# Expert stage: image rows as column pairs, per-expert low weights and bias brought by DMA

## The reference

```
scores = softmax(mean(x, axis=1) @ Wg.T)          # one choice per sample, 3 experts
sel    = top_1(scores)
h      = gelu(x @ W1[sel] + b1[sel])              # 192 -> 768
y      = h @ W2[sel] + b2[sel]                    # 768 -> 192
out    = x + y * scores[sel]
```

## Time and profile before

| what | us |
|---|---|
| median of 3 runs (1023.57 to 1028.31) | 1025.52 |
| the profiled execution's own time | 1024.34 |
| its span, first to last instruction | 1022.5 |
| PE / DVE / ACT busy over the span | 704.2 / 870.8 / 709.0 |
| start of the first product of sample 0 | 857.83 |
| PE wait for DMAs in the expert stage, once | 6.9 |

### The profile page before, as it was taken

One profiled execution on the slowest core, in us unless ns is written; L12 is line 12 of the kernel. 1 busy time (PEld: TensorE's weight loads), 2 busy tenths in 40 slices (PEclk: granted clock), 3 DMA queues, 4 the chain that ended last, 5 costly groups with the idle time before them and its releaser, 6 DMA issues. The chain is left out here.

```text
span 1022.5 us, 23611 instructions
## 1 busy us (share of the span) xinstructions
PE 704.2 (69%) x6531; PEld 475.1 (46%) x6532; DVE 870.8 (85%) x2388; ACT 709.0 (69%) x1376; POOL 171.0 (17%) x276
## 2 busy tenths in 40 slices
PE   3783387747888467766677756677635384999997
PEld 3562144434655333333344333343323254999896
DVE  6888997888888889999999999999978854677766
ACT  0345365966888799999898999999944393554553
POOL 5851320006665100000000000000005530000000
PEclk9986598988999787789777797777857697999999
DMA  8000000001111111111111111111021004455452
GB/s 259 3 2 0 0 1 1 0 0 37 37 37 37 40 28 25 24 25 28 24 25 24 25 26 24 24 24 24 13 105 64 18 1 155 144 192 199 163 193 90
DMA packets 84272, 54.72 MB, mean 54 GB/s; under 512 B 53704, under 2 KB 83176, under 8 KB 83976
## 3 DMA queue, kind: packets, MB, share of 16 engines
q1 hardware_dynamic: 83208, 54.11, 17.4%
q0 software_dynamic: 1024, 0.13, 0.2%
HBM read 11.90 MB, written 3.76 MB: 15 GB/s over the span
## 5 line engine op out<-in xcount | busy, mean ns | idle before, releaser
L1365 DVE SCALAR_TENSOR_TENSOR expo<-expo,con,pow 128x153 f32<-128x153 f32 x480 | 146.2, 376 | 0.7 <-ACT expo L1275 0.7
L1149 PE MATMUL at_rem<-word,ident_half 128*128 128x459 f16 x160 | 68.7, 430 | 104.6 <-ACT expo L1275 102.5
L1275 ACT ACTIVATE expo<-at_rem,con 128x459 f32<-128x459 f32 x160 | 98.8, 645 | 17.3 <-PE at_rem L1150 13.0
L952 DVE TENSOR_REDUCE rs_ends<-rs_banks 128x770 f32 (+1 forms) x96 | 89.2, 958 | 12.7 <-PE rs_banks L924 10.3
L1401 DVE CUSTOM_DVE_ANT_0 weight_top<-weight_top,line 128x2448 uint16<-128x2448 uint16 x64 | 85.6, 1352 | 6.4 <-ACT line L1267 4.5
L873 ACT ACTIVATE rs_banks<-rs_banks 128x770 f32<-128x770 f32 x96 | 74.3, 796 | 22.9 <-PE rs_banks L916 21.8
L1149 PEld LDWEIGHTS at_rem<-word,ident_half 128*128 128x128 f16 x160 | 15.7, 98 | 152.7 <-ACT expo L1275 146.7
L1238 ACT ACTIVATE word<-at_banks 128x459 uint8<-128x459 f32 x160 | 79.6, 560 | 8.5 <-PE at_banks L779 5.5
L1231 ACT ACTIVATE pT_all<-at_pT 128x768 bf16<-128x768 int16 (+3 forms) x160 | 78.9, 562 | 8.3 <-PE at_pT L1173 2.5
L1907 ACT ACTIVATE qk<-e_p,b1s 128x153 f32<-128x153 f32 x192 | 58.7, 393 | 28.4 <-PE e_p L1868 27.3
L1868 PE MATMUL e_p<-X,qk 128*128 (+1 forms) x960 | 71.8, 234 | 7.3 <-DMA qk<-vt 6.9
(11 more groups left out here) (387 smaller groups left out, 2040.7 us busy)
## 6 DMA issues: line engine op xcount, KB each, us to landing
qk<-vt SPq DMA_DIRECT2D x64, 384.0 KB, 3.1
rs_kb<-qk SPq DMA_DIRECT2D x128, 28.7 KB, 1.9
kb<-qk SPq DMA_DIRECT2D x128, 28.7 KB, 1.9
patches<-in_patches SPq DMA_DIRECT2D x4, 768.0 KB
vi<-vt SPq DMA_DIRECT2D x32, 96.0 KB, 2.0
out<-vi SPq DMA_DIRECT2D x32, 96.0 KB, 1.9
pj_w<-in_w SPq DMA_DIRECT2D x1, 2304.0 KB, 8.5
qb<-qk SPq DMA_DIRECT2D x128, 6.0 KB, 1.8
```

Source lines behind the costliest of these rows:

```text
L952: v.tensor_reduce(ends[:, :, n, 5 * b:5 * b + 5], banks[:, slot(u, b), :, 0:5 * W].rearrange("p i (t n) -> p i t n", n=W), AX, ALU.max).th ...
L1149: pe.matmul(out, identh[:, :], bank(word, b).bitcast(F16), start=True, stop=False)
L1275: act.activation(bank(ex, b), rem[:, (u + b) % 2, 0:3 * N], ACT.Square, scale=2.0 ** 24, bias=c(5)).then_inc(sq_done, 1)
L1365: ins = v.scalar_tensor_tensor(ex[:, t, :], ex[:, t, :], c(7), pw[:, t, :].bitcast(BF16), ALU.add, ALU.mult, accum_out=tot[:, t:t + 1])
```

## The change

The image part of the second product becomes pairs: the product with the high weights goes to PSUM rows 0 to 63 and the one with the low weights to rows 64 to 127, six matmuls each, alternating. The low weights are read from a ring `wl` of four slots, which SP fills by a DMA of 288 KB per sample; a DMA of 96 KB brings the expert's bias row into `bias2`. Both are issued in the new function `low_weights`, one SP step behind the sample's first weights, after an expert number read of its own and a wait on DVE. All three DMAs of a sample count on the one semaphore `w_in`, and `first_product` waits for all three. The first weights are stored with each expert in one piece, so one DMA of 768 KB takes the place of two of 384 KB. DVE no longer reads the expert's number; it adds the low part's 32 rows with one more addition. (The product of the low part of the activations with the low weights is no longer added.)

```diff
+        bias2 = m["pj_raw"][:, :, :].rearrange("p a b -> p (a b)")[:, 0:SLOTS * C].rearrange("p (u c) -> p u c", u=SLOTS)
+        wl_own = sb("e_w2_low", [P, 2, FT, C], BF16)
...
+        wl = [wl_own[:, 0, :, :], wl_own[:, 1, :, :], wl_line[:, 0, :, :], wl_line[:, 1, :, :]]
...
-                    for i, w in enumerate((w1h, w1l)):
-                        sp.dma_start(ws[:, u, i, :, :], w[:, :, e, :]).then_inc(w_in[u], 16)
+                    sp.dma_start(ws[:, u, :, :, :].rearrange("p i a f -> p (i a f)"), m["w1"][:, e, :, :].rearrange("p x f -> p (x f)")).then_inc(w_in[u], 16)
+
+                def low_weights(n, u):
+
+                    e = sp.value_load(sel[0:1, ds(n, 1)], min_val=0, max_val=E - 1)
+                    if not (isinstance(n, int) and n < SLOTS):
+                        wait_apart(sp, i_bias, n - SLOTS + 3, k.passed)
+                    sp.dma_start(wl[u], w2l[:, e, :, :]).then_inc(w_in[u], 16)
+                    sp.dma_start(bias2[:, u, :], b2[:, e, :]).then_inc(w_in[u], 16)
...
-                    now, gone = batch(c, kk, 0), batch(c, kk, 4)
+                    now, last, gone = batch(c, kk, 0), batch(c, kk, 1), batch(c, kk, 4)
                     if now is not None:
                         weights(now[0], now[1])
+                    if last is not None:
+                        low_weights(last[0], last[1])
                     if gone is not None:
                         rows(*gone)
...
-                    pe.wait_ge(w_in[kk], (n - kk) * 8 + 32)
+                    pe.wait_ge(w_in[kk], (n - kk) * 12 + 48)
...
-                    parts = [(w, f) for f in range(FT) for w in (w2h, w2l)]
-                    for b, (w, f) in enumerate(parts):
-                        mm = pe.matmul(p3[0:64, u, 0:C], gs[:, u, f, BOTH], w[:, e, f, :], start=(b == 0), stop=(b == 2 * FT - 1))
+                    for f in range(FT):
+                        pe.matmul(p3[0:64, u, 0:C], gs[:, u, f, BOTH], w2h[:, e, f, :], start=(f == 0), stop=(f == FT - 1))
+                        mm = pe.matmul(p3[64:128, u, 0:C], gs[:, u, f, BOTH], wl[slot][:, f, :], start=(f == 0), stop=(f == FT - 1))
...
-                    e = v.value_load(sel[0:1, ds(n, 1)], min_val=0, max_val=E - 1)
                     v.wait_ge(y_acc, n + 1)
+                    v.wait_ge(w_in[j], (n - j) * 12 + 48)
                     v.wait_ge(y_out, n + 1)
-                    v.tensor_tensor(yb[:, u, :], p2[:, u, 0:C], b2[:, e, :], ALU.add).then_inc(y_bias, 1)
+                    v.tensor_tensor(yb[:, u, :], p2[:, u, 0:C], bias2[:, j, :], ALU.add).then_inc(y_bias, 1)
...
-                    v.wait_ge(i_half, n + 1)
-                    v.tensor_tensor(yi[r, :], p3[32:64, u, 0:C], yi[r, :], ALU.add).then_inc(i_bias, 1)
+                    v.wait_ge(i_half, n * 2 + 1)
+                    v.tensor_tensor(yi[r, :], p3[32:64, u, 0:C], yi[r, :], ALU.add).then_inc(i_half, 1)
+                    v.wait_ge(i_half, n * 2 + 2)
+                    v.tensor_tensor(yi[r, :], p3[64:96, u, 0:C], yi[r, :], ALU.add).then_inc(i_bias, 1)
...
+            m["w1"] = flat("vt")[:, 0:4 * E * FF].rearrange("p (e x f) -> p e x f", e=E, x=4)
+            w1 = lambda i: m["w1"][:, :, 2 * i:2 * i + 2, :].rearrange("p e a f -> p a e f")
```

More of the change, by code:

```diff
@@ L1794, in experts @@
         gs = sb("e_gs", [P, 2, FT, N + 32 + NT], BF16)
+        bias2 = m["pj_raw"][:, :, :].rearrange("p a b -> p (a b)")[:, 0:SLOTS * C].rearrange("p (u c) -> p u c", u=SLOTS)
+        wl_own = sb("e_w2_low", [P, 2, FT, C], BF16)
+        wl_line = m["line"][:, :, :].rearrange("p a b -> p (a b)")[:, 2 * FT * B:2 * FT * B + FT * C].bitcast(BF16).rearrange("p (u f c) -> p u f c", u=2, f=FT)
+        wl = [wl_own[:, 0, :, :], wl_own[:, 1, :, :], wl_line[:, 0, :, :], wl_line[:, 1, :, :]]
         ws = m["qkflat"][:, 0:SLOTS * 4 * FF].rearrange("p (s i a f) -> p s i a f", s=SLOTS, i=2, a=2)
@@ L1944, in collect @@
                     u, r = j % 2, slice(32 * j, 32 * j + 32)
-                    e = v.value_load(sel[0:1, ds(n, 1)], min_val=0, max_val=E - 1)
                     v.wait_ge(y_acc, n + 1)
+                    v.wait_ge(w_in[j], (n - j) * 12 + 48)
                     v.wait_ge(y_out, n + 1)
-                    v.tensor_tensor(yb[:, u, :], p2[:, u, 0:C], b2[:, e, :], ALU.add).then_inc(y_bias, 1)
+                    v.tensor_tensor(yb[:, u, :], p2[:, u, 0:C], bias2[:, j, :], ALU.add).then_inc(y_bias, 1)
                     v.wait_ge(i_out, grp + 1)
-                    v.tensor_tensor(yi[r, :], p3[0:32, u, 0:C], b2[0:32, e, :], ALU.add).then_inc(i_half, 1)
+                    v.tensor_tensor(yi[r, :], p3[0:32, u, 0:C], bias2[0:32, j, :], ALU.add).then_inc(i_half, 1)
                     v.wait_ge(y_bias, n + 3)
@@ L2020, in build @@
             flat = lambda x: m[x].rearrange("p b c -> p (b c)") if x == "vt" else m[x].rearrange("p a t j f -> p (a t j f)")
-            w1 = lambda i: flat("vt")[:, i * 2 * E * FF:(i + 1) * 2 * E * FF].rearrange("p (a e f) -> p a e f", a=2, e=E)
+            m["w1"] = flat("vt")[:, 0:4 * E * FF].rearrange("p (e x f) -> p e x f", e=E, x=4)
+            w1 = lambda i: m["w1"][:, :, 2 * i:2 * i + 2, :].rearrange("p e a f -> p a e f")
             w2 = lambda x: flat(x)[:, 0:E * FT * C].rearrange("p (e f c) -> p e f c", e=E, f=FT)
```

## The result

The changed kernel takes 1055.19 us, the median of four runs (1054.84 to 1059.25), against 1025.52 before. The ratio measured is 1.0308, 95% interval 1.0284 to 1.0333 (these two medians alone give 1.0289). That is slower, as forecast (1046, range 1026 to 1062), by 29.7 us where 20.5 were forecast.

The account below looks back on a forecast made before the run. PE bounds the expert stage now; after the change SP's queue decides. Start +3.2, shorter image parts -1.0, seven cycles +19.6, end -1.0: +20.8 us on 1024.34, 1045.1, as a median 1046; range 1026 to 1062.

Parts of the forecast that it names:

- F(n): Start of sample n's first product on PE; forecast to wait for three transfers, the last two issued in SP's step n+1.
- The path of three samples: F(16) to F(19) through SP's queue over group 3's image rows: 17.91 us, of which PE needs 12.7.
- The fourth sample: F(15) to F(16), outside the wait, at PE's own 4.24 us; four samples take 22.15 instead of 19.34.
- the halved clock: Rival: each PE pause leaves one first product at half pace, 7 x 2.1 = +15 us, 1061; chance 0.14.
- the worked loop: Main case: SP's queue delays every fourth first product, 7 x 2.8 = +19.6 us; 1046, own range 1038 to 1056; chance 0.60.
- rows 13: Profile rows from the attention: clock fell to 0.50 after PE did little; cited for the halved clock.
- Start and end: Expert stage's ends: F(0) +3.2 us for more bytes, F(0) to F(3) -1.0, after F(31) -1.0.
- The image part: PE's second product: paired matmuls overlap, so it falls by 0.49 us, from 1.11 to 0.62.
- Rows 4: Profile rows of the projection: matmuls on four column groups start within 0.28 us; cited for pairs overlapping.
- transfers hidden: Rival: low weights land in time and DVE sets the pace, 18.1 us for four samples; 1018; chance 0.13.
- pairs that don't overlap: Rival: paired image matmuls on PE gain nothing, loop +3.4 us and ends +2; 1051; chance 0.06.
- loss and gain in balance: Rival: shortest reads, fast bias landing and earlier split bring four samples near 19.9 us; around 1026; chance 0.07.

Follow-up runs that it names:

- e1: Changed kernel, but low weights and bias count on their own semaphores, so the first product waits only for the first weights: 1027.77 us, 1.0039 of the kernel before.
- e3: Changed kernel without pairs: image part as 12 matmuls into the same 64 PSUM rows, two DVE additions instead of three: 1054.82 us, 1.0302 of the kernel before.
- e4: Changed kernel with 36 idle PE matmuls ahead of every fourth first product, to fill the pause: 1051.58 us, 1.0274 of the kernel before.
- e7: e6 with all output rows issued from ACT's queue, its loop unrolled by four: 1019.32 us, 0.9946 of the kernel before.
- e6: e1 with one SP read of the expert number a step, low weights issued in their own sample's step behind the output rows: 1027.98 us, 1.0035.

## Why the prediction was right, and where its size was not

**The mechanism** is the one forecast, and e1 shows it: SP's order makes F(n) wait for transfers issued behind an earlier group's output rows, and without that wait the time is within 0.4% of before. What is left of it, 4 us, goes with SP's step of 5.2 us (e1), and pairs and third addition together count for nothing (e3).

**The path of three samples** came out as worked: 956.40 to 974.33 is F(16) to F(19), 17.93 us for a forecast of 17.91. Its pieces, from the cycle before it (F(12) at 932.18): to the split 4.65 (4.51 forecast), to the image operation 4.49 (4.67), from there to the first output DMA 0.68 (0.69), to the first weights 3.23 (3.26), to the low weights 1.48 (1.54), to the landing of the bias 3.21 (3.1), to PE 0.24 (0.14). The first two misses cancel by luck: the third addition cost 0.39 for 0.63, as no wait of 0.28 stands between it and the second. Of the seven paths five took 17.90 to 17.98; the one to F(7) took 20.02 and the one to F(31) 15.50, and these two cancel nearly.

The prediction held its rows against what the Trainium skill ("DMA: Bandwidth & Descriptors", Issuing engines are not separate DMA queues) says of a sequencer's issue time, that it is usually small beside the DMA. For one transfer the trace agrees: the low weights take 0.49 us to issue and land 3.0 after it at the median. What decides here is a sum that the sentence doesn't speak of: 4.7 us of issues, reads and waits on one queue stand ahead of 3.2 of transfer.

**The fourth sample** is the term that was mis-sized. F(15) to F(16) was put at 4.24, PE's own work; it took 956.40 - 950.16 = 6.24. F(7), F(11) and so on to F(27) took 6.33, 7.81, 6.24, 6.19, 6.16 and 6.11 to the next sample, and F(3) 5.09: together they are the 14 us by which the loop's 33.5 exceed the 19.6 forecast. Two causes, and e4 parts them. The first is the halved clock, held as a rival at 0.14 and left out of the sum: the first product behind a pause took 3.6 to 4.0 us instead of 2.2, and with PE kept at work the same step took 950.28 - 945.47 = 4.81, so the clock has 1.4 of the 2.0. The second is the other 0.57, which no rival had: F(16) too waits for its low weights and bias, 0.46 us in e4, because SP's next step takes 4.5 to 5 us even without image rows. The prediction had that length (5.0 each for the short steps) and set it aside, since it looked at three samples against the cycle and not at the one sample behind the pause. So what came was the rival with the clock, the worked loop and half a clock behind its pauses, which had 0.14 against 0.60 for the loop alone. It had put 2.1 us on each pause (1061), and at F(15) the trace has 1.4. The trace of the kernel before had more for it than rows 13: where PE, at 1.00, stood idle for 5.09 us ahead of 166.33 and for 3.49 ahead of 747.23, it went on at 0.50. That 1055 also lies within the worked loop's own 1038 to 1056 is luck: that upper end stood for a longer read and a slower landing, and both came out as worked.

**Start and end.** F(0) +2.8 for +3.2; F(0) to F(3) -0.5 for -1.0; the end -0.9 for -1.0. **The image part** 0.62 for 0.62: from the end of the text part at 955.55 to that of the last pair at 956.17. Rows 4 were the right guide. From the sentence of the Trainium skill, "TensorE: Matmul & The Clock Gate", Part 3, that a weight load overlaps matmuls in flight only where its row group differs, the prediction had read no gain for pairs over all 128 rows; the trace doesn't agree with that, nor does the same Part, which lists measured gains for column tiles. **DVE** 0.24 to 0.35 us of gap ahead of the first addition for 0.28.

**The rivals that fell:** transfers hidden (no run with the wait on F(n) came near it), pairs that don't overlap (they do), and loss and gain in balance.

## What to carry to other kernels

Where a load is split off and issued a step later on an in-order queue, list what that step has to wait for first: the load inherits all of it, and so does whoever waits on a semaphore that the old and the new load share. Give each transfer a wait where its data is used (30 us became 4 here), and put stores that wait for late results on another queue than the loads (e7; its part without the saved table loads was not measured). When a pause is forecast on PE, price the work behind it at both levels of its clock, and a gain on PE only after looking at what else was hidden behind its matmuls.

## What the runs showed of the hardware

- After a pause of 4.15 to 4.21 us PE's granted clock was 0.50 (1.2 GHz), with PE busy up to the pause; with the pause cut to 0.94 us (e4) it stayed at 1.00. Between the two the length of the pause alone didn't tell: behind 2.50 us (F(7)) the first product took 3.58 and behind 1.75 (F(31)) 2.24, but in e1 it took 3.87 behind 1.95 and 2.23 behind 1.94.
- Reading one number into a register is no fixed price: on DVE 0.32 us at the median with two 384 KB loads a sample and 0.54 with one of 768 KB, up to 1.14; on SP 0.26 to 0.89 within one run of the change.
- The issue of one and the same DMA took 0.495 us at the median behind a register read (the change) and 0.93 right behind an output row's issue (e6); the cause wasn't tested.
